# Three changes of order in a fused transformer layer: who splits the expert activations, and when

## The reference

```
h = concat(cls, patches @ W + b, txt)
h = h + attention(layernorm(h))            # 12 heads of 16, causal, RMS-normed q and k, rotary
x = layernorm(h)
h = h + shared_ffn(x) + sum_e w_e(x) * expert_e(x)
expert(x)  = (silu(x @ gate) * (x @ up)) @ down      # inner width 384, 3 routed experts
w_e        = two largest of sigmoid(x @ router + bias), divided by their sum
```

## Time and profile before

| what | value |
|---|---|
| median of 3 runs | 1715.58 us |
| profiled execution | 1714.51 us, its span 1712.7 us |
| PE busy | 1565.5 us, 91% |
| DVE, ACT, POOL busy | 1309.9, 1028.9, 913.0 us |
| mean granted TensorE clock | 0.991 |
| POOL `weigh` (L1105), `low_h` (L1111) | 256.6 us of 288; 248.5 us of 279 |
| a turn with two row tiles, with one | 52.4 us, 51.0 us |

### The profile page before, as it was taken

One profiled execution on the slowest core, in us unless ns is written; L12 is line 12 of the kernel. 1 busy time (PEld: TensorE's weight loads), 2 busy tenths in 40 slices (PEclk: granted clock), 3 DMA queues, 4 the chain that ended last, 5 costly groups with the idle time before them and its releaser, 6 DMA issues.

```text
span 1712.7 us, 47747 instructions
## 1 busy us (share of the span) xinstructions
PE 1565.5 (91%) x16472; PEld 1440.5 (84%) x16472; DVE 1309.9 (76%) x3265; ACT 1028.9 (60%) x2314; POOL 913.0 (53%) x1214
## 2 busy tenths in 40 slices
PE   6899999999999999999999999999999999998887
PEld 6688888888898888888888888888888888887777
DVE  6877778777777777787777788777788777787755
ACT  4566655666655666556666656666656666655652
POOL 1366545566445564455665455665455565455561
PEclk8999999999999999999999999999999999999999
DMA  5212221112221122211112211112211111211111
GB/s 208 75 55 73 77 84 49 61 66 74 84 74 45 63 75 77 84 47 58 54 62 72 72 51 53 52 67 65 72 58 50 56 60 65 72 64 36 41 42 32
DMA packets 93512, 112.43 MB, mean 66 GB/s; under 512 B 14049, under 2 KB 78233, under 8 KB 93465
## 3 DMA queue, kind: packets, MB, share of 16 engines
q1 hardware_dynamic: 82904, 91.06, 15.5%
q10 hardware_dynamic: 10560, 20.74, 3.5%
HBM read 48.47 MB, written 12.66 MB: 36 GB/s over the span
## 4 chain that ended last, share of the span: by engine, by line
POOL 42%; issue 41%; PE 10%; DVE 3%; ACT 2%; POOLq 1%; DMA 0%; ACTq 0%; SPq 0%; DVEq 0%
POOL ht L1105 13%; POOL h_low L1111 11%; PE ps L471 9%; POOL probs L1086 8%; POOL probs L1080 4%; POOL rstd L1093 3%; POOL rstd L1095 1%; DVE h_low L1171 1%; POOL rstd L1091 1%; ACT rows L873 1%; PE ps L474 1%; DVE xt L1200 0%; DVE rotated L1217 0%; POOL rstd L1097 0%; DVE crossed L1215 0%
## 5 line engine op out<-in xcount | busy, mean ns | idle before, releaser
L471 PE MATMUL ps<-xt,wf 64*128 64x326 f32 x6912 | 603.1, 316 | 1.3 <-ACT qt L866 0.5
L471 PEld LDWEIGHTS ps<-xt,wf 64*128 64x128 f32 x6912 | 542.9, 186 | 17.6 <-ACT qt L866 10.3
L1080 POOL TENSOR_TENSOR probs<-probs,causal 69x140 f32<-69x140 f32 x192 | 89.0, 464 | 499.6 <-ACT probs L891 499.5
L1086 POOL TENSOR_TENSOR probs<-probs,causal 128x512 f32<-128x512 f32 x192 | 229.0, 1193 | 173.5 <-ACT probs L891 173.4
L1146 DVE SCALAR_TENSOR_TENSOR gated<-tanh_g,ps 128x326 f32<-128x326 f32 x384 | 188.8, 492 | 168.6 <-ACT tanh_g L880 168.0
L873 ACT ACTIVATE rows<-h,rstd 128x192 f32<-128x192 f32 (+2 forms) x279 | 151.1, 564 | 243.2 <-POOL rstd L1097 241.8
L1105 POOL TENSOR_TENSOR ht<-ht,weight_cols 128x326 f32<-128x326 f32 x288 | 256.6, 922 | 25.0 <-DMA weight_cols<-kept_weights 25.0
L880 ACT ACTIVATE tanh_g<-ps 128x326 f32<-128x326 f32 x384 | 169.5, 441 | 165.9 <-PE ps L471 165.4
L891 ACT ACTIVATE probs<-ps 128x792 f32<-128x792 f32 (+1 forms) x384 | 254.5, 663 | 14.4 <-PE ps L471 14.2
L1111 POOL TENSOR_TENSOR h_low<-ht,h_high 128x326 fp32r<-128x326 f32 x279 | 248.5, 921 | 0.0
L471 PE MATMUL ps<-wa_hi,xt 128*128 128x288 f32 (+3 forms) x576 | 159.3, 296 | 74.9 <-DVE xt L1200 74.9
(11 more groups left out here) (126 smaller groups left out, 3065.0 us busy)
## 6 DMA issues: line engine op xcount, KB each, us to landing
kt<-kt SPq DMA_DIRECT2D x384, 40.8 KB, 1.8
weight_cols<-kept_weights SPq DMA_DIRECT2D x32, 489.0 KB, 4.9
x_s<-in_xp ACTq DMA_DIRECT2D x40, 384.0 KB, 4.2
qt<-qt SPq DMA_DIRECT2D x132, 81.5 KB, 1.9
o<-h SPq DMA_DIRECT2D x32, 288.0 KB, 2.4
residual<-h SPq DMA_DIRECT2D x31, 288.0 KB, 2.4
out<-o SPq DMA_DIRECT2D x32, 192.0 KB
qt<-qt ACTq DMA_DIRECT2D x60, 81.5 KB, 2.2
```

What stands on the lines that cost most here:

```text
L471: return nc.tensor.matmul(dst, lhs, rhs, start=first, stop=last)
L1080: nc.gpsimd.tensor_tensor(d, d, shaped(causal[0:REAL2], [[0, 2], [1, COLS2]]), ALU.mult).then_inc(masked.sem, 1)
L1086: nc.gpsimd.tensor_tensor(d, d, shaped(causal[:], [[0, 2], [0, 2], [1, P]]), ALU.mult).then_inc(masked.sem, 1)
```

## The change

GpSimd only weighs: its `low_h` is gone, and five of the nine weighings of a turn stand between the masks of the pairs 3 to 5. VectorE makes all twelve `low_h`: units 0 to 2 after the units 5 to 7 of the first half, 3 and 4 before `keep_low` of `xt`, 5 to 7 before the rotations, 8 before the residual sum, 9 to 11 after the last `rms` step. The rounded part of units 0 to 4 has a place of its own (`h_early`), and ScalarE rounds units 0 to 2 in the first half. The weights are turned and kept one unit earlier, written before SyncE waits for the output stores, and read back in three DMAs, one per expert, each with its own semaphore. At the end of a turn ScalarE copies `out_cols` after the first `qt` and its two DMA issues, and TensorE runs the router before the last two turnings of q and k.

```diff
@@ -64,9 +64,9 @@
 UNITS = FFNS * CHUNKS
 SUMS = 2
 ROUTED = UNITS - CHUNKS
-HIGH_AT = GROUP * (2 * COLS - P + COLS2)
-EARLY_HIGH = 7
-WEIGHTS_UNIT = 5
+EARLY_LOW, MIDDLE_LOW = 5, 9
+LATE_AT = GROUP * (2 * COLS - P + COLS2)
+WEIGHTS_UNIT = 4
 SPLIT_AT = [0, 4, 8, 10, 11, 12]
...
@@ -412,24 +415,30 @@
                 sp.wait_ge(summed.sem, summed.at(b, SUMS))
                 sp.dma_start(out[b, 0:2 * P, :].rearrange("(t p) d -> p t d", p=P), o[:, 0:2, :]).then_inc(stored.sem, 16)
                 sp.dma_start(out[b, 2 * P:TOKENS, :], o[0:REAL2, 2, :]).then_inc(stored.sem, 16)
-                sp.wait_ge(stored.sem, stored.at(b, 32))
+
+            def store_weights(b):
+
+                sp.wait_ge(weights_held.sem, weights_held.at(b, 1))
+                sp.dma_start(weight_rows, weight_held).then_inc(weights_stored.sem, 16)
 
             def spread_weights(b):
 
-                sp.wait_ge(weights_held.sem, weights_held.at(b, 1))
-                sp.dma_start(weight_rows, weight_held[:]).then_inc(weights_stored.sem, 16)
                 if later(b):
                     sp.wait_ge(h_weighted.sem, h_weighted.at(b - 1, ROUTED))
                 sp.wait_ge(weights_stored.sem, weights_stored.at(b, 16))
-                sp.dma_start(weight_cols[:], weight_spread).then_inc(weights_loaded.sem, 16)
+                for e in range(EXPERTS):
+                    sp.dma_start(weight_cols[:, e, :], weight_spread[e]).then_inc(weights_loaded[e].sem, 16)
 
             def turn(i, at, N, D, T, L, A, F):
                 b0, b1, b2, b3 = i + 2, i + 1, i, i - 1
-                sp.wait_ge(h1_ready.sem, h1_ready.at(b3, 1))
                 if later(b3):
                     store_out(b3 - 1)
+                store_weights(b3)
+                spread_weights(b3)
+                if later(b3):
+                    sp.wait_ge(stored.sem, stored.at(b3 - 1, 32))
+                sp.wait_ge(h1_ready.sem, h1_ready.at(b3, 1))
                 sp.dma_start(o[:], h1[:]).then_inc(o_copied.sem, 16)
-                spread_weights(b3)
...
@@ -788,11 +797,14 @@
                 down_rest(range(6, UNITS), b3, A)
                 if L:
                     first_groups(b1)
-                    for n in range(2, 2 * GROUPS):
+                    for n in range(2, 4):
+                        qk_turn(n, b1, at, N)
+                if A:
+                    router(b2)
+                if L:
+                    for n in range(4, 2 * GROUPS):
                         qk_turn(n, b1, at, N)
                 out_turn(b3)
-                if A:
-                    router(b2)
 
...
+            def keep_out(b):
+
+                act.wait_ge(down_done.sem, down_done.at(b, 2))
+                copy(out_cols[:], ps[:, DOWN_BANK:DOWN_BANK + 2, 0:COLS]).then_inc(out_kept.sem, 1)
+
...
@@ -916,6 +933,8 @@
                         tanh(k, b3)
                     if A:
                         exp(k, b2)
+                    if CHUNKS <= k < 2 * CHUNKS:
+                        round_h(range(k - CHUNKS, k - CHUNKS + 1), b3)
                     if N and k == 7:
                         act.wait_ge(embedded.sem, embedded.at(at, 0))
                         for t in range(N):
@@ -933,12 +952,13 @@
                 if A:
                     keep_y(0, b2)
                     keep_y(1, b2)
-                    round_h(range(0, CHUNKS), b3)
+                round_h(range(CHUNKS, EARLY_LOW), b3)
+                if A:
                     keep_y(2, b2)
                 if L:
                     for h in range(2):
                         keep_high(h, xt[:, 2 * h, :], XT_BANK + h, n1_turned, b1, xt_hi)
-                round_h(range(CHUNKS if A else 0, EARLY_HIGH), b3)
+                round_h(range(EARLY_LOW, MIDDLE_LOW), b3)
...
@@ -967,8 +987,8 @@
                 if A:
                     for j in range(BLOCKS):
                         keep_high(j, xt2[:, j, 0, :], N2_BANK[j], n2_turned, b2, xt2_hi)
-                act.wait_ge(down_done.sem, down_done.at(b3, 2))
-                copy(out_cols[:], ps[:, DOWN_BANK:DOWN_BANK + 2, 0:COLS]).then_inc(out_kept.sem, 1)
+                if not L:
+                    keep_out(b3)
                 if L:
                     for g in range(GROUPS):
                         act.wait_ge(qk_turned.sem, qk_turned.at(b1, 2 * g + 1))
@@ -978,6 +998,7 @@
                             act.wait_ge(qt_kept.sem, qt_kept.at(b1, 1))
                             for m in range(2):
                                 act.dma_start(f32(qt[1 - m:P:2, m, :]), f32(qt[m:P:2, m, :])).then_inc(qk_doubled[m].sem, 16)
+                            keep_out(b3)
...
             def turn(i, at, N, D, T, L, A, F):
+                early = iter(range(CHUNKS, UNITS))
                 for p in range(PAIRS):
                     if A:
                         mask_last(p, i)
+                        if p > 3:
+                            weigh([next(early)], i - 1)
                         mask_full(p, i)
+                        if p > 2:
+                            weigh([next(early)], i - 1)
                     if L and p == 2:
                         inverse_root(i + 1, n1_moments, mean_var, rstd, n1_root, n1_ready)
-                for units in (range(CHUNKS, EARLY_HIGH), range(EARLY_HIGH, UNITS)):
-                    weigh(units, i - 1)
-                    if A:
-                        for k in units:
-                            low_h(k, i - 1)
+                weigh(early, i - 1)
                 if A:
                     inverse_root(i, n2_moments, mean_var2, rstd2, n2_root, n2_ready)
...
@@ -1356,17 +1373,21 @@
                     if k == 1:
                         for n in range(3, 7):
                             route_pick(n, b3)
+                    if 5 <= k < 8:
+                        low_h(k - 5, b3)
                     if k == 2 and L:
                         dve.wait_ge(txt_loaded.sem, txt_loaded.at(b1 - 1, 32))
                         dve.wait_ge(hidden_loaded.sem, hidden_loaded.at(b1 - FIRST, 32))
                         moments(h0, stats, stats_chain, b1, rstd, mean_var, n1_moments)
-                for k in range(CHUNKS if A else UNITS):
+                for k in range(CHUNKS, EARLY_LOW):
                     low_h(k, b3)
                 if L:
                     for h in range(2):
                         keep_low(h, xt[:, 2 * h + 1, :], xt[:, 2 * h, :], XT_BANK + h, xt_hi, b1, xt_lo)
                 if A:
                     divide_rows(b2)
+                for k in range(EARLY_LOW, MIDDLE_LOW - 1):
+                    low_h(k, b3)
                 if L:
                     rotate(0, b1)
                     rotate(1, b1)
@@ -1380,6 +1401,7 @@
                     rms_sum(2, b1)
                     for n in range(2):
                         rms_step(n, b1)
+                low_h(MIDDLE_LOW - 1, b3)
                 if A:
                     add_residual(b2)
                     dve.wait_ge(h1_ready.sem, h1_ready.at(b2, 1))
@@ -1387,6 +1409,8 @@
                 if L:
                     for n in range(2, RSQRT_STEPS):
                         rms_step(n, b1)
+                for k in range(MIDDLE_LOW, UNITS):
+                    low_h(k, b3)
                 if N:
                     dve.wait_ge(rows_stored.sem, rows_stored.at(at, 0))
                     embed_sum(at, N)
@@ -1396,10 +1420,9 @@
                         rms_scale(t, b1)
                     for t in range(TILES):
                         low_part(t, b1)
-                    norm2_low(0, b2)
+                    for j in range(BLOCKS):
+                        norm2_low(j, b2)
                     keep_k(0, b1, KEEP_BANK)
-                    norm2_low(1, b2)
-                    norm2_low(2, b2)
```

60 lines of the change are left out of this document (29 added, 31 removed).

## The result

The changed kernel takes 1729.67 us (median of 4 runs, 1729.08 to 1734.03) where the kernel before took 1715.48 beside it (4 runs): ratio 1.009, 95% interval 1.007 to 1.011. It is slower, by 0.9%; 1674 was forecast. The profiled execution's span grew from 1712.7 to 1728.5 us, 15.8 us.

The account below looks back on a forecast made before the run. TensorE was taken as the bound, idle 3.46 us per two-tile turn. 12 x 1.0 + 19 x 1.4 + 2.5 = 41.1 us off 1714.51 gave 1673.4; with the median 1.1 above, 1674, range 1650 to 1699.

Parts of the forecast that it names:

- one contended one less, -1.0 us; it would be ready at 626.6: Before `project_qkv`: VectorE runs two `h_low` instead of three, so `xt` is ready 1.0 us sooner.
- units and scores: First half: `h_low` meets GpSimd's inverse-root chain, delaying the ninth score; 0.4 us lost, bounds 0 and 1.0.
- value: Value matmuls: the third group waits for GpSimd's last mask, a new wait of 0.45 us, bounds 0.2 and 1.2.
- to `project_qkv`: TensorE's 1.10 us wait for `xt` goes; with the new 0.45 wait, 0.65 us is won.
- `project_qkv` to `project_y`: Three more `h_low` cost 1.3 us but rotations shorten to 0.36 each; the whole 1.31 us wait goes.
- end of the turn: `out_cols` comes later behind `qt` and the DMA issues, router covers 0.46; 0.6 us lost, bounds 0.3 and 0.8.
- One-tile turns: Turns with one row tile: VectorE reaches the residual sum sooner, 0.4 us more won than with two tiles, 1.4 in all.
- Whole-instruction exclusion: Rival, chance 0.13: ahead of the inverse root GpSimd loses 0.486 for each of two meetings, 1.0 not 0.4 a turn: 1693.
- the contended row: Profile row cited against exclusion: GpSimd's weighing takes 0.770 us alone, 1.018 beside two-operand VectorE instructions, 0.25 a meeting.
- More is won: Rival, chance 0.19: first-half meeting and late `out_cols` cost only lower bounds, 0 and 0.3; 0.7 more a turn, 1653.
- The wait only moves: Rival, chance 0.08: three `h_low` ahead of the rotations run stretched, `project_y` waits as now; about 1714, no change.
- Slower: the weights come late: Rival, chance 0.09: GpSimd waits for weights before the first weighing, TensorE for the last mask; 1.85 a turn lost, 1772.

Follow-up runs that it names:

- r_one_gap: The changed kernel with the weighing of unit 8 alone waiting for that of unit 7: 1645.38 us, ratio 0.9585 to the kernel before.
- p_probe: The changed kernel plus 39 idle-chip trials behind its last turn, one VectorE `h_low` against a GpSimd batch: none held, `h_low` took 0.43 to 1.08 us.
- l_gap_low_h_later: The changed kernel with each weighing from unit 8 waiting for the one before, and `h_low` of units 0 to 2 behind units 7 to 9: 1713.38 us.
- k_best: The changed kernel with stops from unit 7, last masks ahead of weighings 6 and 7, `h_low` 0 to 2 later, old end of turn: 1664.03 us.
- t_probe_longer: The changed kernel plus 84 trials with TensorE loaded, GpSimd batches of 16, arrivals 3.5 to 11 us: all 24 from 8.9 us on held.

## Why the prediction was wrong

**The step that failed** is "one contended one less, -1.0 us; it would be ready at 626.6". It priced a meeting of `h_low` and a weighing by how they took turns in the earlier trace rows, 0.96 us each, whatever GpSimd had done before. The change fills GpSimd's waits between the masks with weighings, so it comes to the meeting after 8.1 us without a stop, and then VectorE is let in only when the batch has ended. The first `h_low` costs 3.7 us and not 1.0.

What it cost is read off one stop against none, after against `r_one_gap`, TensorE's projections in both:

```profile
L481 PE MATMUL ps<-wa_hi,xt 128*128 128x288 f32 (+3 forms) x576 | 169.8, 313 | 62.4 <-DVE xt L1217 62.4
L481 PE MATMUL ps<-wb,xt 128*128 128x288 f32 (+3 forms) x576 | 127.0, 304 | 0.0
L481 PE MATMUL ps<-wa_lo,xt 128*128 128x288 f32 (+3 forms) x288 | 88.0, 305 | 0.0
```

```profile
L481 PE MATMUL ps<-wa_hi,xt 128*128 128x288 f32 (+3 forms) x576 | 158.1, 294 | 2.6 <-DVE xt L1219 2.6
L481 PE MATMUL ps<-wb,xt 128*128 128x288 f32 (+3 forms) x576 | 119.3, 289 | 0.0
L481 PE MATMUL ps<-wa_lo,xt 128*128 128x288 f32 (+3 forms) x288 | 83.2, 289 | 0.0
```

The wait is 59.8 us less and the matmuls 24.2 less busy: 84.0 of the 85.1 us between the spans. Most of the 24.2 is the half clock (an estimate: ten stretches of some 1.5 us, by the turns of 54.5 against 53.0).

**The other terms**, TensorE's timeline of a two-tile turn cut at the same places in before and `r_one_gap`, where the hold is gone:

| stretch | before | one stop | change | forecast |
|---|---|---|---|---|
| units and scores | 20.53 | 20.96 | +0.43 | +0.4 |
| value | 3.41 | 3.91 | +0.50 | +0.45 |
| norm turnings behind value | 0.80 | 0.62 | -0.18 | 0 |
| to `project_qkv` | 1.79 | 0.54 | -1.25 | -1.10 |
| `project_qkv` to `project_y` | 7.93 | 6.42 | -1.51 | -1.31 |
| end of the turn | 3.80 | 4.25 | +0.45 | +0.6 |
| whole turn, the rest within 0.05 | 52.42 | 50.82 | -1.60 | -0.96 |

The mechanisms held; the sizes erred mostly one way. The two stops that went had cost 0.15 and 0.20 more than their waits, the one that came in `value` costs 0.13 less than forecast with the turnings behind it, and the end of the turn 0.15 less. VectorE's rotations did fall, to 0.358 us. One-tile turns won 2.15 (51.0 to 48.85) where 1.4 was forecast. Turns 29 to 31, which I counted as one-tile turns, won 4.0, 2.5 and 5.8, and the last turn 3.5 (38.6 to 35.1, counted from its first unit to the end of the span) for 2.5. So with one stop in it, and the hold gone, the kernel comes out at 1645, below my range: the range was too narrow on that side as well.

*The rivals.* "Whole-instruction exclusion" named the two engines but not the event. By the Trainium skill's rule ("SBUF — State Buffer", section "SBUF: two separate sides") whichever instruction starts first has the shared ports for the whole of it, and the other waits for that one. The trials in `p_probe` agree for a single meeting, and they show that taking turns whole costs GpSimd 0.25 and not 0.486, so the contended row was no evidence against the rule. The trace of after doesn't agree: `h_low` waited out the running weighing and four more. The rival was also priced at another meeting, the inverse root, where the score's wait came out at 0.97, within the forecast's 0.8 to 1.2. "More is won" (1653) came nearest to the 1645 of one stop, but not by its terms, 0 and 0.3: they came out at 0.43 and 0.45. "The wait only moves" put the stretched `h_low` ahead of `project_y`, where there is no wait left. "Slower: the weights come late" did not happen: they are written at 628.41 and read from 630.27, and GpSimd does not wait for them. What I missed was to ask of GpSimd what I asked of the others: when does it next stand still?

**What stays open.** What in the chip does the holding; what sets its onset between 4.2 us and 10; why one began 2.4 us after a stop in `l_gap_low_h_later` and `k_best`, and why it ended there at a boundary and not at a stop. In 61 of these 62 holds it was the last boundary ahead of GpSimd's next stop, of 0.8 to 1.1 us; in after, `h_low` was not let in at that boundary. The size of the meeting at the inverse root by itself was not measured, because of that hold.

## What to carry to other kernels

Where VectorE and GpSimd both work on SBUF, look not only at how long a meeting takes but at how long GpSimd has run without a stop when VectorE comes: filling its last gaps turned a 1 us meeting here into one that lasted for the rest of its batch. It is no safe rule, since `l_gap_low_h_later` was held soon after a stop; so read the duration of each such VectorE instruction after the change. One wait on its own preceding instruction, put where VectorE arrives, gave 84 us here for 0.5 us of GpSimd's time a turn. And where an engine ahead of TensorE slips by 2 us, count the clock too: nine of twelve such waits in two-tile turns cost another 1.5 us.

## What the hardware showed

A VectorE subtraction with two SBUF inputs can be passed over at up to eleven boundaries between GpSimd's instructions (9.2 us in `t_probe_longer`). In after and in the trials it ended 0.36 us after GpSimd's last instruction; in `l_gap_low_h_later` and `k_best` it ended 0.35 to 0.40 us after one inside the batch. In `r_one_gap` a stop on GpSimd, 0.08 us between two rows that otherwise overlap by 0.04 (its next instruction waits for its last), let it in.

A single meeting in `p_probe` goes by whole instructions. `h_low` ended 0.35 us after the GpSimd instruction in which it came (0.43 us long by itself), and where it came first, GpSimd's first instruction ended 0.62 us after it, 1.01 to 1.35 us long instead of 0.76. Memsets on VectorE stood ahead of it there, but no cost of theirs to GpSimd shows: the 0.62 is the same for memsets of 16 to 320 columns, and where 480 or 640 columns of memset put `h_low` later, GpSimd's first instruction took 0.76.
